# VectorE writes the zeros into a bank of sums, in place of TensorE's product of zeros, in a graph network's second phase

## The reference, cut to what matters

```
for l in range(3):
    f1 = relu(x[row] @ nb_W[l] + nb_b[l]);  f2 = relu(x[col] @ self_W[l] + self_b[l])
    h = relu(concat([f1, f2]) @ att1_W[l] + att1_b[l])
    mask = clip(sigmoid(h @ att2_W[l] + att2_b[l]) * 1.5 - 0.45, 0, 1)
    d = clip((segment_sum(mask, row) + 1e-6) ** -0.5, 0, 10)
    x = segment_sum((mask * d[row] * d[col])[:, None] * x[col], row)
    out = out + x
```

## Time and profile before

| what | value |
|---|---|
| time, median of 3 runs (lowest to highest) | 9091.96 us (9091.9 to 9094.2) |
| span of the profiled execution | 9111.0 us |
| VectorE busy in the whole span | 74% |
| TensorE products busy in the whole span | 62% |
| phase B | three stretches of about 650 us, from about 2764, 5580 and 8395 us on |

### The profile page before, as it was taken

The page is one execution under the profiler, slowest core; times in us unless marked ns, Lnnn a source line. Parts: engine busy times, 40 slices in busy tenths (PEclk is TensorE's granted clock), DMA queues, the critical chain, the costliest instruction groups (busy, mean ns, idle before and its releaser), DMA issues.

```text
span 9111.0 us, 203370 instructions
## 1 busy us (share of the span) xinstructions
PE 5650.8 (62%) x43467; PEld 5151.5 (57%) x43630; DVE 6736.5 (74%) x29039; ACT 3666.1 (40%) x8663; POOL 5960.7 (65%) x6294
## 2 busy tenths in 40 slices
PE   3135555555558996555555557998555555555996
PEld 1135555545548885555555556887555555555886
DVE  8877777777777877777777777877777777776788
ACT  0013322322227883322322325885322322323886
POOL 0017777777775656777777776665777777776664
PEclk7565555555558996555555557998555555555998
DMA  1014444444456664444444446665444444445665
GB/s 24 0 48 135 132 130 131 132 130 130 133 128 206 213 206 130 132 131 130 132 130 131 132 130 176 210 212 156 132 130 130 133 130 131 132 130 146 213 211 161
DMA packets 1122388, 1272.27 MB, mean 140 GB/s; under 512 B 648596, under 2 KB 652724, under 8 KB 1122356
## 3 DMA queue, kind: packets, MB, share of 16 engines
q1 hardware_dynamic: 922676, 903.51, 32.1%
q0 software_dynamic: 199680, 368.45, 16.7%
HBM read 868.11 MB, written 403.23 MB: 140 GB/s over the span
## 4 chain that ended last, share of the span: by engine, by line
POOL 44%; issue 23%; PE 22%; DVE 8%; DMA 1%; ACT 1%; POOLq 0%; DVEq 0%; ACTq 0%; SPq 0%
POOL got L526 22%; PE bank L552 12%; POOL k_hot L526 11%; POOL g_hot L526 10%; PE bank L685 6%; DVE acc L946 2%; DVE acc L947 2%; PE bank L653 1%; PE bank L690 1%; PE bank L610 1%; PE bank L601 1%; PE bank L576 1%; DMA k_x<-kept_x 1%; DMA k_hot<-qx_table,index 0%; DVE acc L909 0%
## 5 line engine op out<-in xcount | busy, mean ns | idle before, releaser
L653 PE MATMUL bank<-p_all,onehot_t 128*128 x10032 | 2301.5, 424 | 1752.4 <-issue 1731.8
L653 PEld LDWEIGHTS bank<-p_all,onehot_t 128*128 128x128 f32 x10032 | 2186.8, 330 | 1803.4 <-issue 1803.4
L526 POOL DMA_INDIRECT got<-qx_table,index x2496 | 2376.4, 952 | 784.9 <-issue 780.3
L539 POOL DMA_INDIRECT got<-y_table,index x1248 | 1187.3, 951 | 798.8 <-issue 431.5
L798 ACT ACTIVATE small<-small 128x8 f32<-128x8 f32 x624 | 130.2, 209 | 3813.9 <-DVE small L1080 3813.9
L526 POOL DMA_INDIRECT k_hot<-qx_table,index x1248 | 1181.3, 947 | 393.7 <-issue 377.5
L526 POOL DMA_INDIRECT g_hot<-qx_table,index x1248 | 1185.6, 950 | 380.6 <-issue 380.6
L552 PE MATMUL bank<-mask,onehots 128*128 128x3 bf16 x4992 | 669.8, 184 | 986.1 <-DVE mask L1091 986.1
L552 PEld LDWEIGHTS bank<-mask,onehots 128*128 128x128 bf16 x4992 | 516.0, 104 | 1250.7 <-issue 1145.5
L1118 DVE SCALAR_TENSOR_TENSOR p_all<-iota_b,col_hi,bank 128x104 f32<-128x104 bf16 x3768 | 953.9, 317 | 341.5 <-PE bank L685 335.4
L1056 DVE TENSOR_SCALAR onehots<-iota_b,rows_b 128x128 bf16<-128x128 bf16 x5016 | 888.7, 280 | 48.0
(11 more groups left out here) (167 smaller groups left out, 8859.7 us busy)
## 6 DMA issues: line engine op xcount, KB each, us to landing
onehot_t<-look_hot SPq DMA_DIRECT2D x474, 256.0 KB
row_hot<-onehots SPq DMA_DIRECT2D x468, 256.0 KB, 3.6
k_x<-col_rows SPq DMA_DIRECT2D x318, 256.0 KB, 3.6
kept_x<-got SPq DMA_DIRECT2D x312, 256.0 KB
look_hot<-k_x SPq DMA_DIRECT2D x312, 256.0 KB, 2.1
hot_in<-row_hot SPq DMA_DIRECT2D x312, 256.0 KB
k_x<-kept_x SPq DMA_DIRECT2D x312, 256.0 KB
look_new<-row_hot SPq DMA_DIRECT2D x159, 256.0 KB
```

The source lines that it names most:

```text
L526: pool.indirect_dma_start(got[j][:, k, :], None, qx_table, bass.IndirectOffsetOnAxis(ap=index[j][:, k:k + 1], axis=0)).then_inc(a_got[j], 16)
L539: pool.indirect_dma_start(got[j][:, k, 0:HID], None, y_table, bass.IndirectOffsetOnAxis(ap=index[j][:, k:k + 1], axis=0)).then_inc(g_got[j ...
L653: last = mm(bank_p[h][:, k, :], onehot_t[h][:, k, :], p_all[:, ds(ids[k], 1), :].rearrange("p o d -> p (o d)"), start=True, stop=True)
```

## The change

Four products of zeros per quad leave TensorE's loop. Instead, each join on VectorE is followed by a wait for its own end (a new semaphore `k_read`) and by a memset of the bank to zero; the semaphore that tells TensorE that the bank is free now comes from the memset. Before the loop TensorE clears all four banks of sums once per layer.

```diff
 def sum_edges(to, hot, rows, there, ready, half, after):
-    clear(to)
     pe.wait_ge(*there)
+    pe.sem_inc(pe_go, 1)
...
     for j in range(2):
         pick_rows(0, j)
+    for i in (0, 1, 3):
+        clear(bank[i])
     clear(bank[2]).then_inc(k_o[2], 1)
...
-def join(blk, sums):
+def join(blk, sums, read, n):
     first = dve.snap(blk, min_val=0, max_val=BLOCKS - 1)
     some = acc[:, ds(first, U), :].rearrange("p b d -> p (b d)")
-    return v.tensor_tensor(some, some, sums[:, :], ALU.add)
+    v.tensor_tensor(some, some, sums[:, :], ALU.add).then_inc(read, 1)
+    dve.wait_ge(read, n)
+    return v.memset(sums[:, :], 0.0)
...
-    join(k_blk, bank[(i - 1) % 3]).then_inc(k_acc[(i - 1) % 3], 1)
+    join(k_blk, bank[(i - 1) % 3], k_read[(i - 1) % 3], nth(l, b * 2, i - 1)).then_inc(k_acc[(i - 1) % 3], 1)
...
-            join(g_blk, bank[3]).then_inc(g_acc, 1)
+            join(g_blk, bank[3], k_read[3], l * QUADS + (b * 2 + (i // 3 + 1))).then_inc(g_acc, 1)
```

More of the change, by code:

```diff
@@ L280, in build @@
             [sem(f"{name}{c}") for c in range(3)] for name in ("a_colin", "a_look", "a_lookst", "k_lookin", "k_xin", "k_o"))
-        t_zero, a_hotst = sem("t_zero"), two("a_hotst")
+        t_zero, a_hotst, k_read = sem("t_zero"), two("a_hotst"), four("k_read")
         k_hotin, k_cast = ([sem(f"{name}{c}") for c in range(3)] for name in ("k_hotin", "k_cast"))
```

## The result

The changed kernel takes 9372.91 us (9336.87 to 9382.59, three runs) against 9091.96: a ratio of 1.0297, interval 1.0269 to 1.0325. The direction was forecast; the size was not: the time lies 113 us above the 9260 us and 28 above the range.

The account below looks back on a forecast made before the run. TensorE was taken to pace the quad now, with VectorE having only 1.89 us of waits to spare and becoming the bound. 137 - 8 + 39 = 168 us on 9092 gave 9260 us, range 9157 to 9345.

Parts of the forecast that it names:

- VectorE becomes the bound: Phase B: both VectorE waits for TensorE's picks vanish, and VectorE paces the quad with its sequencer last; chance 0.72.
- The new quad: VectorE's path through one phase B quad, summed piece by piece: 13.23 us against 12.35, +0.88 per quad, +137 us.
- The sequencer stays ahead: Rival: VectorE's register work behind the memset still runs under the join; +0.47 us per quad, 9157 us; chance 0.08.
- the wait is free: Rival: a semaphore between two VectorE instructions costs nothing; +0.11 us per quad, about 9101 us; chance 0.03.
- I take one in five quads or so, 0.25 us per quad, +39 us.: Phase B: assumed frequency of 3.4 us stretches with TensorE at half clock, and their cost.
- The bound of 1.35 us per quad, 210 us: Phase B: cost if a 3.4 us half-clock stretch of TensorE came once per quad, 0.35 us slack taken off.
- The clock goes down and stays down: Rival: TensorE's clock stays low in phase B; down half the time, some 9092 + 400 us; chance 0.09.
- Four products of zeros per quad, worth 0.88 us at most: TensorE in phase B: most that removing the products frees, 4 x 0.22 us per quad, 137 us in all.
- Faster: Rival: zeros written in 0.25 us and VectorE's sequencer keeping up; -0.53 us per quad, 9010 us; chance 0.05.
- the 4.40 and 4.55 us of TensorE's side: TensorE's time without products of zeros, one-hot array to step 2's look-ups and from there to the next look-ups.
- the slack of 0.35 and 0.53 us: How much later VectorE reaches two look-ups than TensorE's side, at 4.75 and 5.08 us, so both waits vanish.
- 137 - 8: Phase B: +137 us from VectorE's longer quad, less 8 us for half of today's 0.11 us stalls vanishing.

Follow-up runs that it names:

- e2: The kernel before, products of zeros kept, with only a wait for the join's own end behind each join, no memset: 9280.87 us, ratio 1.0192.
- e3: The changed kernel with the k groups' wait and memset moved behind the weigh and the load of the next block: 9127.55 us, ratio 1.0023.
- e5: The changed kernel with two products of zeros ahead of each sum, into a bank nothing reads, eight per quad: 9284.24 us, ratio 1.0198.
- e4: The kernel before without the products of zeros in the loop and nothing in their place, banks not emptied: 9116.39 us, ratio 1.0011.
- e10: The kernel before with the weigh ahead of the join and no products of zeros in the loop, banks not emptied: 9071.75 us, ratio 0.9972.
- e8: The changed kernel as it is, run again beside the others on one chip: 9338.67 us, ratio 1.0253 to the kernel before.
- e1: The changed kernel with one product of zeros ahead of each sum, into a bank nothing reads, four per quad: 9286.47 us, ratio 1.0197.
- e6: The changed kernel with the weigh moved ahead of the join and memset, three weight buffers instead of two: 9506.80 us, ratio 1.0441.
- e11: The kernel before with a memset into an unused bank behind each join, without a wait, products of zeros kept: 9190.13 us, ratio 1.0101.

## Why the prediction was right in its direction and wrong in its size

Of the 113 us, the clock is 64, the loop's turn 23, and 21 are the distance of the two profiled executions to their medians; the rest is small.

- **VectorE becomes the bound: right.** "The new quad" was summed to 13.23 us; quiet quads inside a body take 13.34. The parts are near, too: the memset starts 0.86 us after the join (forecast 0.71), takes 0.48 (0.50), and from its start it is 0.62 us to the one-hot array (0.74), 0.88 to the look-ups of step 2 (0.95), 1.07 to the g join (1.20) and, behind the g group, 0.39 to the look-ups (0.50). That the sum is so close is part luck: the four waits were sized 0.6 us too short in all (0.18 us behind a join's end, not 0.03), the four stretches behind them 0.4 too long. The register work does wait for the join's end: e2 has the loss without a memset, e3 the memset without the loss. *The sequencer stays ahead* and *the wait is free* fall with e2. The Trainium skill (VectorE: DVE Perf Modes, The DRAIN you can't avoid) has eight copies take the same time with a semaphore after each as with one after the last. That does not carry over to this kernel, whose sequencer has register work behind the wait: e2 is 175 us slower by such waits alone.
- **The clock: the step that failed.** "I take one in five quads or so, 0.25 us per quad, +39 us." In the profiled execution 59 of 150 quads had a fall, two in five. In 36 of them it lasted 3.4 us or less, and these cost about 0.5 us each, 18 in all, against the 1.35 forecast. The other 23 were at 1.2 GHz for 6.8 to 14.5 us (17 of them 10.2), most in runs one behind another, and cost about 3.7 us each, 85 in all; the forecast had no such quads. Set against the quiet quads of their kind all 59 cost 103 us. The bound of 1.35 us per quad, 210 us, was written down and then cut to a fifth by nothing but the quads of today, which have less idle time; the range's upper end (0.6 x 1.35 x 156 = 126 us) still had room for the true size, the value did not. *The clock goes down and stays down* came about in part: in runs of quads of 17 us TensorE was the bound again (15.73 us busy of 17.03). The Trainium skill (TensorE: Matmul & The Clock Gate, A second HAM failure mode: psum-queue depth-cycling) tells of a kernel whose clock swung, by small idle gaps of TensorE, and lost throughput. This trace agrees on the swing and the loss, with 17.03 us where 13.34 stood; that small gaps bring the falls on is not shown, though e5, with products in them, has 5 falls in place of 48.
- **The loop's turn: left out.** The sum went around one quad as if the loop did not turn. Before, the turn lay under a wait, so no row of it looked like a cost; the step that removed the wait took its cover away. 0.31 us more across a turn than before, 75 times, 23 us.
- **"Four products of zeros per quad, worth 0.88 us at most": the bound held, but the value is zero** (e4, e10). *Faster* could not have come about, whatever the memset's price: e4 has neither products of zeros nor memsets in the loop and gains nothing. For the same reason the 4.40 and 4.55 us of TensorE's side, and the slack of 0.35 and 0.53 us worked out from them, counted on time that taking the products out does not free.
- **The account.** 0.96 us in 150 quads makes 144, the turn 23, the clock 103; less 7 for the falls of before and 7 in the layers' first quads (their sum fell from 68.4 us to 61.3): 256 of the 260 us of span. With both 7s, VectorE's part is 130, against 137 - 8 in the forecast. The medians differ by 281 us, since the profile of before lay 19 us above its median and the one after 2 below; the forecast had taken the span's change for the median's. How far the time misses is also chance: e8, the same kernel in another group, took 9338.67 us, inside the range, with 48 falls.

What stays open: when the clock falls, and why in runs of 17 us quads. The kernels show more falls with fewer products (e8, e1, e5) and with slower quads (e6), and few in quads of 12.4 us without any product of zeros (e3, e4); that is not a rule. Nor was e11's late weigh tried by itself.

## What to carry to other kernels

Before adding a wait for an engine's own previous instruction, list the register work and loads that its sequencer does under that instruction; if they come next in line, they become the path, and the same wait behind them cost next to nothing here (e3). Time on the chain is not time to be gained: a product that stands on it can lie over the sequencer's own work, and taking it out shows that (e4). When a change turns the bound from TensorE to another engine, price the clock with the full bound that rows give, and look for what the vanished waits had covered, loop turns among it.

## What was not expected of the hardware

- A memset of 128x512 fp32 in PSUM has a row of 0.48 us, starts 0.18 us after the join's row ends when it waits for it, and lets the next instruction start 0.39 us after its own start.
- A loop body of VectorE written for four quads instead of two appears to have its code loaded anew at each turn: 248 packets of instruction code in place of 26, and some 5 us per turn (18.7 us against 13.75).
- The clock of one and the same kernel fell in 59 quads of one execution and in 48 of another, with 1.0297 and 1.0253 of the time before.
